# A four-stage model kernel: head values normalized in stage 2, the last stage moved into the last Mamba step, one PSUM bank of z changed, the silu block moved by one unit

## The reference, cut to what matters

```python
# block 0: differential attention, 8 heads of 16 values, then the output projection
y = einsum(A1 - lambda_full * A2, v)                        # per head
y = y * rsqrt(mean(y * y, -1) + 1e-5) * subln_weight        # norm within a head
y = y * (1.0 - 0.5)
s = y @ Wo.T + bo
# its ffn: z = LN(y + moe(y)), 8 experts, one for each token; b2[e] is added by the expert's mask
x = x + s * silu(z)
# block 1: four Mamba layers
for i in range(4):
    xi, z = split(x @ in_w.T)
    xc = silu(conv(xi) + cb)
    dt, B, C = split(xc @ xp_w.T)
    h = exp(delta * A) * h + (delta * xc) * B ; y = sum(h * C) + xc * D    # 16 states a channel
    x = (y * silu(z)) @ out_w.T
# its ffn: top-2 mixture of 8 experts plus a shared expert; its sum is GATE below, before the silu
x = x + s * silu(ffn(xn))
```

## Time and profile before

| | us |
|---|---|
| median of 3 runs | 1451.6 |
| the runs | 1446.62, 1451.6, 1455.39 |
| the profiled execution, its own time | 1447.76 |
| span of its trace, first to last instruction | 1446.0 |
| busy in the span: PE, DVE, ACT, POOL | 1231.7, 1123.5, 1046.5, 960.0 |
| mean granted TensorE clock | 0.941 |

### The profile page before, as it was taken

The page is one execution under the profiler, slowest core; times in us unless marked ns, Lnnn a source line. Parts: engine busy times, 40 slices in busy tenths (PEclk is TensorE's granted clock), DMA queues, the critical chain, the costliest instruction groups (busy, mean ns, idle before and its releaser), DMA issues. The chain is left out here.

```text
span 1446.0 us, 21389 instructions
## 1 busy us (share of the span) xinstructions
PE 1231.7 (85%) x6427; PEld 609.4 (42%) x6427; DVE 1123.5 (78%) x1598; ACT 1046.5 (72%) x1812; POOL 960.0 (66%) x916
## 2 busy tenths in 40 slices
PE   6367699999329999889999999999999999999884
PEld 4351144444325566534344434444444444444331
DVE  7857588887576222259999999999999999999985
ACT  4337699998242223269889989898989898989861
POOL 7652211111653623338999999999999999999983
PEclk9787799999658999999999999999999999999988
DMA  2022133432108104234234423441344243423301
GB/s 63 31 82 98 56 104 121 121 114 86 36 35 304 35 22 124 71 108 104 65 86 102 102 63 77 97 117 61 80 96 107 64 92 90 100 60 90 88 8 59
DMA packets 89710, 123.57 MB, mean 85 GB/s; under 512 B 17142, under 2 KB 48577, under 8 KB 89225
## 3 DMA queue, kind: packets, MB, share of 16 engines
q1 hardware_dynamic: 83048, 103.92, 27.2%
q0 software_dynamic: 6560, 18.44, 4.3%
HBM read 96.18 MB, written 26.92 MB: 85 GB/s over the span
## 5 line engine op out<-in xcount | busy, mean ns | idle before, releaser
L2263 DVE TENSOR_TENSOR_SCAN hs<-decay,dbx 128x512 f32<-128x512 f32 x512 | 588.6, 1203 | 39.7 <-ACT decay L2148 21.5
L1844 POOL TENSOR_TENSOR hcm<-hs,Cc 128x1024 f32<-128x1024 f32 x192 | 452.3, 2367 | 19.3 <-DVE hs L2263 11.7
L2148 ACT ACTIVATE decay<-dtr,a_cur 128x512 f32<-128x512 f32 x512 | 351.0, 710 | 8.2 <-DVE hs L2263 7.8
L1965 PEld LDWEIGHTS dbx<-ident_sb,scaled 128*128 128x128 f32 x1536 | 176.2, 142 | 258.4 <-DVE hs L2263 139.4
L1965 PE MATMUL dbx<-ident_sb,scaled 128*128 128x128 f32 x1536 | 242.9, 282 | 30.4 <-DVE hs L2263 29.4
L2126 ACT ACTIVATE scaled<-duT,BT 128x256 f32<-128x256 f32 x506 | 224.6, 496 | 12.1 <-PE dbx L1965 12.0
L1837 POOL TENSOR_TENSOR hck<-hs,Cc 128x512 f32<-128x512 f32 x128 | 163.6, 1278 | 44.9 <-DVE hs L2263 42.3
L1962 PE MATMUL dbx<-du,spread_sb 128*128 128x512 f32 x256 | 140.4, 631 | 2.8 <-DVE hs L2263 2.8
L907 ACT ACTIVATE ex<-tt 128x1024 f32<-128x1024 f32 x128 | 137.3, 1072 | 4.0 <-DVE tt L957 2.6
L1892 PE MATMUL slots<-XT,w_tap 128*128 128x512 f32 (+1 forms) x240 | 123.3, 601 | 2.3 <-PEq L1294 2.3
L1827 POOL TENSOR_SCALAR scaled<-duT,BT 128x256 f32<-128x256 f32 x256 | 117.6, 478 | 0.0
(11 more groups left out here) (343 smaller groups left out, 1998.9 us busy)
## 6 DMA issues: line engine op xcount, KB each, us to landing
dtr<-dt_turn SPq DMA_DIRECT2D x60, 512.0 KB, 8.4
Cc<-bc_turn SPq DMA_DIRECT2D x256, 64.0 KB, 2.0
dt_turn<-dt SPq DMA_DIRECT2D x15, 512.0 KB, 2.8
Bb<-bc_turn SPq DMA_DIRECT2D x64, 64.0 KB, 2.0
conv_row<-in_conv_row SPq DMA_DIRECT2D x4, 512.0 KB, 5.9
shares_of_tokens<-zeros SPq DMA_DIRECT2D x2, 1024.0 KB, 9.6
w_rg<-in_w_rg SPq DMA_DIRECT2D x8, 256.0 KB
w_ru<-in_w_ru SPq DMA_DIRECT2D x8, 256.0 KB
```

What stands on the lines that cost most here:

```text
L1844: nc.gpsimd.tensor_tensor(hcm[:, (m - 1) % MR:m % MR + 1, :], hs[:, q % HR:p % HR + 1:p - q, :], Cc[:, k:k + 1, :].broadcast_to([P, 2, 512 ...
L1965: last = nc.tensor.transpose(dbx[bank_of[p]][:, P * kk:P * kk + P], scaled[:, (b + k) % 2, kk, g, :, :].rearrange("p j c -> p (j c)"), ide ...
L2148: nc.scalar.activation(dec[:, p % DR, :], dtr[:, b % 2, g, :], ACT.Exp, scale=a_cur[:, 4 * g + k:4 * g + k + 1]).then_inc(s_dec, 1)
L2263: nc.vector.tensor_tensor_scan(hs[:, p % HR, :], dec[:, p % DR, :], dbx[bank_of[p]][:, :], 0.0, ALU.mult, ALU.add).then_inc(s_sc, 1)
```

## The change

Four edits.

1. Stage 2 gets `norm_head`: heads 0 to 6 are divided, joined, squared and reduced by six DVE instructions each, at steps 5 to 10 (the odd head of a pair, not in the first pair) and 21 to 26 (the even one). The root is left to stage 3, which does the six steps for head 7 alone; ACT's squares go. `b2blk`, `sub_col` and `ms` are kept across stages, and the clearing and the 24 small DMAs move from stage 3 to stage 1.
2. z's half 0 goes into `slot[0]` instead of `slot[1]`, and waits for one silu of x instead of two.
3. ACT's silu block stands behind the decay of unit 1 instead of unit 0.
4. Stage 6 is gone. silu of `GATE` is in the first Mamba block, the load of x goes into the free half of `dtr` during block (3,3), batches 0 to 2 are turned, multiplied and added between the units of block (3,3), and stored at once; batch 3 comes after the last output.

```diff
+                        for h in range(NH):
+                            sp.dma_start(sub_col[16 * h:16 * h + 16, :], A["subln"].rearrange("(d o) -> d o", o=1)).then_inc(s_b2l, 16)
+                        sp.wait_ge(s_b2z, 1)
+                        for t in range(NT):
+                            sp.dma_start(b2blk[NE * t:NE * t + NE, t, :], A["b2"]).then_inc(s_b2l, 16)
...
+                        nc.gpsimd.memset(b2blk[:, :, :], 0.0).then_inc(s_b2z, 1)
...
+                        def norm_head(h, n, settled, done):
+                            seg = ybig[:, :, bass.ds(h * 34, 34)].rearrange("p t (s c) -> p t s c", s=2)
+                            plus, minus = seg[:, :, 0, 0:16], seg[:, :, 1, 0:16]
+                            if n == 0:
+                                dve.wait_ge(s_yb, settled)
+                                nc.vector.reciprocal(rz[:, :, :].unsqueeze(3), seg[:, :, :, 16:17]).then_inc(s_hn, 1)
+                                return
+                            dve.wait_ge(s_hn, done + n)
+                            if n == 1:
+                                nc.vector.tensor_scalar(rz[:, :, 1], rz[:, :, 1], neg_lam[:, :], None, ALU.mult).then_inc(s_hn, 1)
+                            if n == 2:
+                                TT(seg[:, :, :, 0:16], seg[:, :, :, 0:16], rz[:, :, :].unsqueeze(3).broadcast_to([P, NT, 2, 16]), ALU.mult).then_inc(s_hn, 1)
+                            if n == 3:
+                                TT(plus, plus, minus, ALU.add).then_inc(s_hn, 1)
+                            if n == 4:
+                                TT(ysq[:, :, :], plus, plus, ALU.mult).then_inc(s_hn, 1)
+                            if n == 5:
+                                nc.vector.tensor_reduce(ms[:, :, bass.ds(h, 1)], ysq[:, :, :].unsqueeze(2), AX.X, ALU.add).then_inc(s_hn, 1)
+
                         def pair_of_heads(q, first=False):
                             for st in range(STEPS):
                                 u, mb = st // 4, st % 4
                                 sums(q, st)
+                                if 5 <= st < 11 and not first:
+                                    norm_head(q * 2 + 1, st - 5, unit(q, 0), q * 12 + 6)
+                                if 21 <= st < 27:
+                                    norm_head(q * 2 + 2, st - 21, unit(q, 4), q * 12 + 12)
...
-                        for i in range(2):
-                            act.wait_ge(s_yv, i + 1)
-                            nc.scalar.activation(half(y2, i), half(yv, i), ACT.Square).then_inc(s_sq, 1)
...
-                        pe.wait_ge(s_b2, 16 * (NT + NH))
...
+                        seg = ybig[:, :, 34 * NH - 34:34 * NH].rearrange("p t (s c) -> p t s c", s=2)
+                        plus, minus = seg[:, :, 0, 0:16], seg[:, :, 1, 0:16]
+                        link(nc.vector.reciprocal(rz[:, :, :].unsqueeze(3), seg[:, :, :, 16:17]))
+                        link(nc.vector.tensor_scalar(rz[:, :, 1], rz[:, :, 1], neg_lam[:, :], None, ALU.mult))
+                        link(TT(seg[:, :, :, 0:16], seg[:, :, :, 0:16], rz[:, :, :].unsqueeze(3).broadcast_to([P, NT, 2, 16]), ALU.mult))
+                        link(TT(plus, plus, minus, ALU.add))
+                        link(TT(ysq[:, :, :], plus, plus, ALU.mult))
+                        link(nc.vector.tensor_reduce(ms[:, :, NH - 1:NH], ysq[:, :, :].unsqueeze(2), AX.X, ALU.add))
+                        nc.vector.tensor_scalar(ms[:, :, :], ms[:, :, :], 1.0 / 16, 1e-5, ALU.mult, ALU.add).then_inc(s_ms, 1)
+                        link(nc.vector.tensor_scalar(sub_col[:, :], sub_col[:, :], 0.5, None, ALU.mult), s_yv)
+                        dve.wait_ge(s_rms, 1)
+                        link(nc.vector.reciprocal(ms[:, :, :], ms[:, :, :]))
...
+                    sp.wait_ge(s_dec, at(3, 3, UN, 0))
+                    sp.dma_start(x_last, x_dram).then_inc(s_x6, 16)
+                    for b in range(B):
+                        sp.wait_ge(s_r6, 2 * b + 2)
+                        sp.dma_start(out[b].rearrange("(k p) d -> p k d", p=P), x_last[:, 4 * b:4 * b + 4, :]).then_inc(s_o6, 16)
+                    sp.wait_ge(s_o6, 16 * B)
...
-                            pe.wait_ge(s_xc, at(l, n + 1, 2, 2))
+                            pe.wait_ge(s_xc, at(l, n + 1, 2, 1))
                         e = 256 + P * h
-                        mm(slot[1 + h][:, :], w_in[:, e:e + P], XT[:, n % 4, :], start=True, stop=True).then_inc(s_z, 1)
+                        mm(slot[2 * h][:, :], w_in[:, e:e + P], XT[:, n % 4, :], start=True, stop=True).then_inc(s_z, 1)
...
+                            if l == 3 and b == 3 and v in (3, 6, 24):
+                                turn_out((3, 6, 24).index(v))
+
+                    def turn_out(b):
+                        pe.wait_ge(s_out, at(3, b, 1, 1))
+                        if b < 2:
+                            pe.wait_ge(s_zs, at(3, 3, 1, 1))
+                        else:
+                            pe.wait_ge(s_r6, 2 * b - 3)
+                        for t in range(4):
+                            last = nc.tensor.transpose(slot[turn_slot[b]][:, P * t:P * t + P], XT[:, b, P * t:P * t + P], ident[:, :])
+                        last.then_inc(s_t6, 1)
...
-                        nc.scalar.activation(zs[:, b % 2, :, :], slots[:, 1:3, :], ACT.Silu).then_inc(s_zs, 1)
+                        nc.scalar.activation(zs[:, b % 2, :, :], slots[:, 0:3:2, :], ACT.Silu).then_inc(s_zs, 1)
...
-                            if w == 0 and not first(l, b):
+                            if w == 1 and not first(l, b):
...
+                                act.wait_ge(s_fin, 4)
+                                nc.scalar.activation(GATE[:, :, :], GATE[:, :, :], ACT.Silu).then_inc(s_g6, 1)
...
+                            if l == 3 and b == 3 and u in (9, 14, 29):
+                                gate_out((9, 14, 29).index(u))
...
+                    def gate_out(b):
+                        tl = slice(4 * b, 4 * b + 4)
+                        dve.wait_ge(s_t6, b + 1)
+                        dve.wait_ge(s_g6, 1)
+                        TT(GATE[:, tl, :], slot[turn_slot[b]].rearrange("p (t d) -> p t d", d=D), GATE[:, tl, :], ALU.mult).then_inc(s_r6, 1)
+                        dve.wait_ge(s_r6, 2 * b + 1)
+                        dve.wait_ge(s_x6, 16)
+                        TT(x_last[:, tl, :], x_last[:, tl, :], GATE[:, tl, :], ALU.add).then_inc(s_r6, 1)
...
+                    gate_out(3)
```

More of the change, by code:

```diff
@@ L1059, in build_stages @@
                 with nc.Block() as block:
-                    @block.sync
-                    def _(sp):
-                        for h in range(NH):
-                            sp.dma_start(sub_col[16 * h:16 * h + 16, :], A["subln"].rearrange("(d o) -> d o", o=1)).then_inc(s_b2, 16)
-                        sp.wait_ge(s_z0, 1)
-                        for t in range(NT):
-                            sp.dma_start(b2blk[NE * t:NE * t + NE, t, :], A["b2"]).then_inc(s_b2, 16)
                     @block.gpsimd
@@ L1199, in _ @@
                         yf = yv[:, :, :].rearrange("p t (h d) -> p (t h) d", d=16)
[L1200 removed]
+                        mf = ms[:, :, :].rearrange("p t h -> p (t h)")
                         rows = lambda i: slice(NT * NH // 2 * i, NT * NH // 2 * (i + 1))
                         for i in range(2):
[L1203 removed]
@@ L1204, in _ @@
-                        dve.wait_ge(s_b2, 16 * (NT + NH))
-                        link(nc.vector.tensor_scalar(sub_col[:, :], sub_col[:, :], 0.5, None, ALU.mult), s_yv)
-                        for i in range(2):
-                            dve.wait_ge(s_sq, i + 1)
-                            last = nc.vector.tensor_reduce(ms[:, rows(i)], y2f[:, rows(i), :], AX.X, ALU.add)
-                        link(last)
-                        nc.vector.tensor_scalar(ms[:, :], ms[:, :], 1.0 / 16, 1e-5, ALU.mult, ALU.add).then_inc(s_ms, 1)
@@ L1211, in _ @@
-                        dve.wait_ge(s_rms, 1)
-                        link(nc.vector.reciprocal(ms[:, :], ms[:, :]))
-                        dve.wait_ge(s_yv, 2)
-                        for i in range(2):
-                            TT(yf[:, rows(i), :], yf[:, rows(i), :], ms[:, rows(i)].unsqueeze(2).broadcast_to([P, NT * NH // 2, 16]), ALU.mult).then_inc(s_yv, 1)
+                            TT(yf[:, rows(i), :], y4[:, rows(i), 0, 0:16], mf[:, rows(i)].unsqueeze(2).broadcast_to([P, NT * NH // 2, 16]), ALU.mult).then_inc(s_yv, 1)
@@ L1676, in build_stages @@
             s_gath = sem("shares_loaded")
+            s_g6, s_t6, s_r6, s_x6 = map(sem, ("gate_ready", "s_by_token", "x_steps", "x_loaded"))
+            s_o6 = sem("out_stored")
+            x_last = dtr[:, 0, 0:4, :].rearrange("p a (t d) -> p (a t) d", d=D)
+            turn_slot = (1, 0, 1, 0)
             main = [(k, g) for k in range(DIRECT) for g in range(8)]
@@ L2060, in _ @@
                         out_proj(3, 3, h)
+                    turn_out(3)
```

65 lines of the change are left out of this document (14 added, 51 removed).

## The result

| | before | changed |
|---|---|---|
| median of 4 runs, us | 1453.32 | 1439.15 |
| the runs, us | 1446.62 to 1455.39 | 1434.85 to 1440.87 |
| ratio, with its 95% interval | | 0.9911 (0.9884 to 0.9937) |
| profiled execution's span, us | 1446.0 | 1438.6 |

The changed kernel is 0.9% faster, 13 us of 1453. The forecast of 1438 us is 1 us from the median. The two spans differ by only 7.4 us: the traced execution of before took 1447.76 us, 5.6 under its median, and that of the changed kernel 1440.87, the slowest of its four.

The account below looks back on a forecast made before the run. PE bounds stage 2, stage 3 is a chain, stage 5 waits for decays, stage 6 ends last. Terms -9.0 + 3.3 + 0.6 + 1.8 + 3.0 - 11.3 = -11.6 on 1447.8 gave 1436.2, forecast as 1438, range 1424 to 1447.

Parts of the forecast that it names:

- Stage 3, -9.0 forecast: Stage 3: b2 matmuls wait for maskT alone and start 9.0 us earlier; -9.0 us, with 5.6 as lower bound.
- everything from y's transposes on moves by 9.0: Stage 3: yv is ready before the b2 matmuls are through, so all later work comes 9.0 us earlier.
- Norms in stage 2, +3.3 forecast: Stage 2: seven heads' norms fit only partly into DVE's idle time; +3.3 us, bounds 0 and 17.
- 0.7 a head (4 heads): Stage 2's loop: each norm costs 0.7 us, with register instructions of 0.5 to 0.6 us and no room left.
- The turns, +0.6 forecast: Stage 5: the earlier decay is spent waiting before times_b; fifteen turns at 0.04 us, +0.6 us, bounds 3 us either side.
- Rival A: Stage 5: unit 1's scan and all behind it come 1.1 us earlier each turn, giving 1419 us; chance 0.11.
- silu of GATE, +1.8 forecast: First Mamba block: 1.91 us more on ACT delays copy_dbc and dt; +1.8 us, bounds 0 and 1.9.
- Block (3,3) and the end, -8.3 forecast: Block (3,3) pays +3.0 us for work moved into it; dropping stage 6 gives -11.3 us.
- DVE waits half a product on average, 1.2: Block (3,3): if DVE's two-SBUF-input sums and POOL's products exclude each other, DVE waits 1.2 us and POOL 0.7.
- rival C: Block (3,3): sums and POOL's products each wait a whole instruction, 9.2 us instead of 1.7, giving 1444; chance 0.08.
- Rivals B: Stage 2: DVE becomes the bound, norms cost 17 us instead of 3.3, giving 1450, no change; chance 0.08.
- rival D: Stage 2: PE's waits for late sums lower its clock, costing some 6.5 us a unit, so slower; chance 0.04.

Follow-up runs that it names:

- norms_late: Changed kernel with no norm in stage 2, stage 3 doing all eight heads as before but with b2blk already loaded; 0.9937 of before, stage 3 54.2 us.
- b2_load_late: Changed kernel with only the clearing of b2blk and the 24 small DMAs back at the start of stage 3; 1.0000 of before, stage 3 62.1 us.
- z_bank_and_psum: Changed kernel with the silu block back behind unit 0's decay and gate_out's product left in PSUM; 0.9807 of before.
- old_turn: Changed kernel with both edits of the Mamba block turn taken back (z's half 0 in slot 1, silu block behind unit 0's decay); 0.9966 of before.
- sum_from_psum: Changed kernel with gate_out's product left in PSUM, so the sum reads one input from PSUM and one from SBUF; 0.9910 of before, 0.9923 when run again.
- gate_silu_last: z_bank_and_psum with the silu block behind unit 1's decay in block (3,3) alone and silu of GATE moved to the last turn; 0.9823 of before.
- after_again: The changed kernel run once more, unaltered, on the chip of the stage 3 experiments; 0.9919 of before.
- after: First trace of the changed kernel itself, compared with before; span 1438.6 us, ratio of the kernel 0.9911.

## Why the prediction was right, point by point

- **Time.** 1438 forecast, 1439.15 measured; the change of 11.6 us on one execution stands against 7.4 and 8.4 us trace against trace and 13 (9 to 17) by the ratio. The sign and size held, but the terms did not. Against the sum of -11.6 the first pair of traces has -7.4: 5.2 too little at the end, 2.0 lost in stage 4 and 1.3 in stage 1, and in return 2.7 more than forecast in stage 3 and 1.4 in stage 2. The median is nearer than that because the traced execution of before was 5.6 us under its median and that of the changed kernel 1.7 above. That the forecast met the median to 1 us is luck.
- **Stage 3, -9.0 forecast, -11.7 and -12.6 measured: the step "everything from y's transposes on moves by 9.0" failed.** The b2 matmuls and the first of y's transposes moved by 9.0 and 9.1. Behind them PE gained more than that (Wo's matmuls 15.7 us earlier), so the bound passed to POOL's indirect DMAs, the chain I had named as the other one. Its end moved by 5.1, and DVE had three of four sums of z done by the time the factors came, where it had one before: that is the other 6.6. The first indirect DMA at 1.4 instead of 4.8 us, which I priced, is part of it. With b2 early, the norms are worth 3.9 to 4.8 us (norms_late against the changed kernel); early b2 alone is worth 7.8.
- **Norms in stage 2, +3.3 forecast: they cost 0.0; mis-sized was "0.7 a head (4 heads)" for the loop.** Stage 2 as a whole is 1.9 and 1.8 us longer, but from the eighth settle to the last all thirteen traces have 174.4 us, with norms or without. b2_load_late and z_bank_and_psum have the norms, and their stage 2 is as long as that of norms_late (261.9 and 261.7 against 262.0). The 1.08 us of idle a unit took the steps in the loop too. The long unit before the loop (9.30 us) goes with a granted clock of 0.59 and 0.52; it is in both traces of the changed kernel, weaker in old_turn and sum_from_psum (8.56 and 8.48), and in none of the other seven with the norms. Why the clock fell there is open.
- **Stage 1, 0 forecast, +1.3 and +0.2 measured**: held as far as it can be told. The shortest stage 1 with the 24 DMAs is 0.1 to 0.2 us longer than the two without.
- **The turns, +0.6 forecast, +0.5 measured.** The argument held in each part: the lead of the early decay is spent before `times_b`, and the early z pays for the late silus. Rival A is out.
- **silu of GATE, +1.8 forecast, +1.7 measured** (46.9 against 45.1), and taken back whole by gate_silu_last. In four of the eleven traces with the silu in this place the block took 48.6 to 48.8 us instead of 46.9. In after_again the granted clock was 0.72 in the 12 us from 646.1, in `after` 1.00 at the same place; before and gate_silu_last, without the silu there, have 1.00. That is another 1.7 to 1.9 us that I hadn't counted.
- **Block (3,3) and the end, -8.3 forecast, -3.1 and -5.6 measured: mis-sized was the price of the lock, "DVE waits half a product on average, 1.2".** The sums cost 10.7 us of DVE time in one trace and 6.7 in the other instead of 3 x 0.69. DVE waits for the end of the running product, and where it comes 0.2 us before that end, until POOL's run of products is over. sum_from_psum shows what this was worth: 6 to 10 us. Sums with both inputs in SBUF did stand in stage 5 before, L2246 ahead of the first block, but POOL ran no product beside them, so no row of before showed the price. This was rival C, to which I gave 0.08, and it came at about its price; that the time came out as forecast all the same is due to stages 2 and 3 and to the luck named under the time.
- **Stage 4**, +2.0 and +3.6 with an unchanged program, is the spread of executions: 211.0 to 216.2 us with the change, 212.6 in the one trace without.
- Rivals B and D are out: in the loop and the last pair a head's two units took 14.9 us as before, which leaves no room for DVE as the bound or for a fallen clock. The one unit with a fallen clock, in the first pair, cost 1.5 us and not the 6.5 of rival D.

## What to carry to other kernels

Two edits that are each read as a gain from the profile can be one zero: walk the engines' programs from the place where a wait goes to the next wait of the same engine, and ask which chain that one follows. Undo them one at a time, since the better half may be worth more alone: here 0.58 us a turn, 7.5 us in all. When a time comes out as expected, add up the stages all the same: twice here the total was right and its parts were not. And before an elementwise sum of two SBUF operands is put between POOL's products, give it one operand from PSUM; a free-looking 0.7 us instruction took up to 6.6.
